# A decoder layer on one core: the first batch's work in another order, and expert 0's tokens prepared one step earlier

## What is computed

```python
h = x * rsqrt(mean(x * x) + 1e-6) * norm_w
q, k, v = heads(h @ Wq.T), heads(h @ Wk.T), heads(h @ Wv.T)   # 8 heads of 64, rope on q and k
beta, ig, og = sigmoid gates of h                             # per token and head
M = M * beta + ig * scale * outer(k, v);  y = (q @ M) * og    # scan over tokens
x = layernorm(x + y @ Wout.T + bout)
r = 0.9 * r + ctx * ctx                                       # scan over each batch's tokens
x = layernorm(x + x * r)
xn = layernorm(x) * gamma + beta                              # 8 experts, 512 tokens each
x = layernorm(x + gelu(xn @ w1[e] + b1[e]) @ w2[e] + b2[e])
```

## Time and profile before

| | us |
|---|---|
| median of 3 runs (lowest, highest) | 1338.41 (1337.49, 1339.36) |
| the profiled execution | 1336.99 |
| its span, first to last instruction | 1334.8 |
| TensorE busy | 1294.9 (97%) |
| VectorE, GpSimd, ScalarE busy | 758.3 (57%), 682.3 (51%), 506.0 (38%) |
| mean granted clock of TensorE | 0.985 |

### The profile page before, as it was taken

One profiled execution on the slowest core, in us unless ns is written; L12 is line 12 of the kernel. 1 busy time (PEld: TensorE's weight loads), 2 busy tenths in 40 slices (PEclk: granted clock), 3 DMA queues, 4 the chain that ended last, 5 costly groups with the idle time before them and its releaser, 6 DMA issues.

```text
span 1334.8 us, 17886 instructions
## 1 busy us (share of the span) xinstructions
PE 1294.9 (97%) x6330; PEld 1015.0 (76%) x6330; DVE 758.3 (57%) x1256; ACT 506.0 (38%) x723; POOL 682.3 (51%) x405
## 2 busy tenths in 40 slices
PE   4799999999999999979999999999999999999998
PEld 3677777777777777757888888888888888888886
DVE  3888888888888888883334342343333433432424
ACT  4333333333333333364343443534333434334330
POOL 1644555445455555436627438537465284375561
PEclk6899999999999999989999999999999999999999
DMA  6433322333333332413413506206125053071220
GB/s 201 137 111 112 105 91 97 104 111 111 111 111 111 111 111 81 174 47 120 165 64 130 194 0 236 88 8 252 64 95 201 26 191 131 0 260 64 68 91 31
DMA packets 108588, 150.69 MB, mean 113 GB/s; under 512 B 10112, under 2 KB 52096, under 8 KB 108544
## 3 DMA queue, kind: packets, MB, share of 16 engines
q1 hardware_dynamic: 108544, 150.10, 33.2%
HBM read 133.16 MB, written 16.92 MB: 112 GB/s over the span
## 4 chain that ended last, share of the span: by engine, by line
PE 84%; DVE 6%; issue 5%; DMA 2%; ACT 1%; POOL 0%; SPq 0%; DVEq 0%; POOLq 0%; ACTq 0%
PE qk_ps L84 8%; PE qk_ps L86 8%; PE qk_ps L85 8%; PE v_ps L84 5%; PE v_ps L86 5%; PE v_ps L85 5%; PE gate_ps L84 4%; PE gate_ps L86 4%; PE gate_ps L85 4%; PE y_ps L86 3%; PE y_ps L85 3%; PE s_ps L84 3%; PE y_ps L84 3%; PE s_ps L86 3%; PE s_ps L85 3%
## 5 line engine op out<-in xcount | busy, mean ns | idle before, releaser
L772 POOL TENSOR_TENSOR rot<-rot 128x1024 f32<-128x1024 f32 x32 | 88.3, 2758 | 188.5 <-DVE rot L951 188.5
L850 POOL TENSOR_TENSOR w_lo<-w_raw,w_hi 128x2048 fp32r<-128x2048 f32 x31 | 143.4, 4626 | 73.0 <-ACT w_hi L655 72.8
L842 POOL TENSOR_TENSOR w_lo<-w_raw,w_hi 128x2048 fp32r<-128x2048 f32 x32 | 147.8, 4619 | 20.5 <-ACT w_hi L665 20.5
L926 DVE TENSOR_TENSOR_SCAN decays<-f_all,diag 128x384 f32<-128x384 f32 x128 | 152.6, 1243 | 0.6
L1082 DVE CAST yT_hi<-v_ps 128x512 fp32r<-128x512 f32 x62 | 42.9, 692 | 182.8 <-ACT v_ps L688 182.8
L1082 DVE CAST yT_hi<-gate_ps 128x512 fp32r<-128x512 f32 x62 | 42.9, 692 | 182.0 <-ACT gate_ps L688 182.0
L84 PE MATMUL qk_ps<-wqkv_hi,xT_parts 128*128 128x512 f32 x256 | 108.2, 422 | 9.8 <-DVE wqkv_lo L888 9.8
L688 ACT ACTIVATE gate_ps<-gate_ps,b_cols 128x512 f32<-128x512 f32 x64 | 42.2, 660 | 190.4 <-PE gate_ps L86 190.4
L814 POOL TENSOR_TENSOR rstd_b<-mean_var_b,ln_eps_b 128x4 f32<-128x4 f32 x15 | 3.0, 202 | 212.6 <-DVE mean_var_b L1070 212.6
L84 PE MATMUL v_ps<-xnT_hi,w_hi 128*128 128x512 f32 x256 | 102.1, 399 | 0.0
L86 PE MATMUL qk_ps<-wqkv_hi,xT_parts 128*128 128x512 f32 x256 | 101.9, 398 | 0.0
(11 more groups left out here) (226 smaller groups left out, 3170.0 us busy)
## 6 DMA issues: line engine op xcount, KB each, us to landing
w_raw<-in_w SPq DMA_DIRECT2D x64, 1024.0 KB, 7.4
f_all<-f_dram SPq DMA_DIRECT2D x16, 1024.0 KB, 4.8
xT_raw<-in_xT SPq DMA_DIRECT2D x16, 512.0 KB, 6.0
x_both<-in_x SPq DMA_DIRECT2D x16, 512.0 KB, 4.8
f_all<-f_dram SPq DMA_DIRECT2D x16, 512.0 KB, 5.9
c_both<-in_ctx_in SPq DMA_DIRECT2D x16, 512.0 KB, 6.5
x_dram<-res SPq DMA_DIRECT2D x16, 512.0 KB, 7.3
x_both<-x_dram SPq DMA_DIRECT2D x8, 1024.0 KB, 5.3
```

What stands on the lines that cost most here:

```text
L772: pool.tensor_tensor(a, a, rot_b[j], ALU.add).then_inc(rot_done, 1)
L842: pool.tensor_tensor(w2_lo[s % 2][:], w2_raw[s % 2][:], w2_hi[s % 2][:].bitcast(F32), ALU.subtract)\
L850: pool.tensor_tensor(w1_lo[s % 2][:], w1_raw[s % 2][:], w1_hi[s % 2][:].bitcast(F32), ALU.subtract)\
L926: dve.tensor_tensor_scan(decays[:, n, :], f_all[:, n, :], diag[:], 0.0, ALU.mult, ALU.add).then_inc(decay_done, 1)
```

## The change

Start of the program. The three gate weights come as one array, as do their biases (nine DMAs for the constants, x and turned x become four ahead of the v weights, with x behind those). Batch 0's rms is not stored and read back: two matmuls against the identity (`first_rms`, behind batch 0's first v product) spread it into the free half of `gate_ps`. The q and k weights are issued right behind x, and rope's table ahead of k's. ScalarE casts v, squares x, casts q, and does the gate between the second and third k piece. In batch 0 VectorE gates v and applies rope for both halves before any scan; two scans follow, then batch 1's gate sums, then six scans and the output weights. TensorE turns batch 0's second half one share later, and its first scores another share later. GpSimd's `residual` of batch 0 stands behind both rotations, that of batch 1 at the front of step 1.

Last batches. Expert 0's tokens are loaded one step earlier, their statistics stand on VectorE between the first and second weighing of step 15, and they are normalized, turned and split in step 15, between the halves of `project_out` and behind it. Both first up products stand in the odd slots of step 16. Batch 15 uses the banks of any other batch. Tiles move with it: `xn` lies on `xT_parts0`, the first w1 slab on `f_all` (loaded behind the last scan), the second on `rot`. The order in steps 2 to 14 is as before.

```diff
-            sp.dma_start(normw[:], norm_w).then_inc(const_in, 16)
             load_xT(Step(0))
-            load_x(Step(0))
-            for g in range(3):
-                sp.dma_start(wg_raw[:, :, g * NH:(g + 1) * NH], wgT[g].rearrange("(k p) n -> p k n", p=P)).then_inc(const_in, 16)
-                sp.dma_start(gate_bias[g * NH:(g + 1) * NH, :], bg[g].rearrange("(n a) -> n a", a=1)).then_inc(const_in, 16)
+            sp.dma_start(normw[:], norm_w).then_inc(const_in, 16)
+            sp.dma_start(wg_raw[:], wgT.rearrange("(k p) n -> p k n", p=P)).then_inc(const_in, 16)
+            sp.dma_start(gate_bias[:], bg).then_inc(const_in, 16)
...
             load_w(2)
-            store_rms(Step(0))
+            load_x(Step(0))
             load_w(0)
-            spread_rms(Step(0))
+            sp.dma_start(rope_sb[:], rope.rearrange("(j p) c -> p j c", p=P)).then_inc(rope_in, 16)
             load_w(1)
+            sp.dma_start(memory_raw[:], decay).then_inc(tables_in, 16)
...
             body(Step(B - 2))
+            sp.wait_ge(xb_done, B)
+            sp.wait_ge(x2_stored, 16 * (B - 3))
+            load_tokens(Step(0))
             body(Step(B - 1))
...
-            load_w1(ahead, 0)
             sp.wait_ge(gates_turned, last.after(1, 1))
             sp.wait_ge(f_stored, last.after(16, 16))
             load_w2(ahead, 0)
+            sp.wait_ge(decay_done, last.after(NH, NH))
+            load_w1(ahead, 0)
+            sp.wait_ge(qk_turned, last.after(2 * NT, 2 * NT))
+            load_w1(ahead, 1)
+            load_w2(ahead, 1)
+            body(Step(B))
...
-                if b.n == B:
-                    expert_normalize(Step(0), 0)
-                    act.wait_ge(e_const_in, 16 * 3)
-                    token_high(Step(0), 0)
-                    token_high(Step(0), 1)
...
+                    if b.n == B - 1 and c == 2:
+                        expert_normalize(Step(0), 0)
+                    if b.n == B and c in (1, 3):
+                        gelu(Step(0), c // 2)
+                    if b.n == B and c == 0:
+                        split_w2(Step(0), 0)
                 if b.n == -1:
                     weights_high(2)
+                    square_x(b + 1)
+                    weights_high(0)
...
                 if b.n == B - 1:
+                    act.wait_ge(e_const_in, 16 * 3)
+                    token_high(Step(0), 0)
+                    token_high(Step(0), 1)
                     split_w1(Step(0), 0)
+                    token_high(Step(0), 2)
+                    token_high(Step(0), 3)
+                    keep_qkT(b, 1)
...
+                if b.n == 0:
+                    dve.tensor_tensor(gates_sum[:], gate_ps[0:NG, L:2 * L], gates_sum[:], ALU.mult).then_inc(gates_summed, 1)
...
+                    if b.n == B and n == 5:
+                        split_hidden(Step(0), 0)
+                    if b.n == B - 1 and n == 1:
+                        expert_stats(Step(0), 0)
...
                         rope_parts(b, 0)
+                        if b.n == 0:
+                            gate_v(b, 1)
+                            rope_parts(b, 1)
                         clear_f(b)
                     if b.within(B):
                         for m in SCANS.get(n, ()):
-                            if b.n != 0 or n != NH - 1:
+                            if b.n != 0 or m < 2:
                                 scan(b, m)
...
+                    for j in range(NT):
+                        add_residual(b - 1, j)
+                        if b.n == B - 1:
+                            token_low(Step(0), 2 * j)
+                            token_low(Step(0), 2 * j + 1)
+                    norm_stats(b - 1, 0)
                 if b.n == 0:
+                    for m in range(2, NH):
+                        scan(b, m)
                     weights_low(3)
...
+            def first_rms():
+                pe.wait_ge(rms_done, 1)
+                for j in range(NT):
+                    mm = pe.matmul(gate_ps[0:NG, L + j * P:L + (j + 1) * P], rms[:, 0, j:j + 1].broadcast_to([P, NG]),
+                                   ident[:], start=True, stop=True)
                 mm.then_inc(gates_ps, 1)
...
+                if b.n == 0 and g == KC:
+                    first_rms()
...
+                if b.n == B and n % 2 == 1:
+                    for k in (n // 2 * 2, n // 2 * 2 + 1):
+                        up(Step(0), k // KC, k % KC)
...
+                    if b.n == B - 2 and b.i is None and j == 1:
+                        turn_tokens(Step(0), 0)
+                        turn_tokens(Step(0), 1)
...
+                if b.n == B - 1:
+                    turn_tokens(Step(0), 2)
+                    turn_tokens(Step(0), 3)
```

186 lines of the change are left out of this document (81 added, 105 removed).

## The result

The changed kernel takes 1330.84 us, the median of 5 runs (1327.37 to 1331.16), where the kernel before took 1337.98 (5 runs, 1337.49 to 1339.36): a ratio of 0.9936, 95% interval 0.9923 to 0.9949 (the quotient of the two medians, 0.9947, lies inside it). It is faster, by 7.1 us and not by the 16 forecast, and its time lies above the range. Timed once more beside other kernels it had 1331.73 against 1338.85, ratio 0.9951 (0.9938 to 0.9964).

The account below looks back on a forecast made before the run. TensorE was taken to lose time only at the start (16.5 us idle) and the hand-over to the first expert (9.1 idle). 1336.99 − 12.2 − 4.4 = 1320.4, 1321.8 against the median, forecast 1322; range 1316 to 1329.

Parts of the forecast that it names:

- start: what goes: Batch 0's start: q-weight wait goes; v starts near 11.1, k products 20.9, projections end at 32.8 (45.55 before).
- Start: what is late next: Batch 0's second scores wait for VectorE's chain of rope, scans, gate sums and weighings: 51.5 where it was 65.10.
- rival 1: Start: VectorE blocked, all six scans at 1.85 or batch 1's rms rows late; term 1 is 7.5, 1326.5; chance 0.16.
- Term 1: Start, batch 0 and start of batch 1: 12.2 us gained, bounds 7.5 and 15.
- Term 2: Hand-over from last batches to first expert: 4.4 us gained, bounds −1 and 9.
- (a): Step 15: VectorE's statistics of expert 0's tokens delay the weighing; TensorE pays 1.5 us (0 to 3.5).
- (b): Last batches: first w1 slab, loaded later, is split on ScalarE ahead of token blocks and keys; 2.4 us (0 to 4.20).
- (c): Step 16: VectorE does batch 14's memory before weighing the second pair; costs 0.8 us.
- (d): Step 16: ScalarE's x2 scaling, w2 split and gelu table delay second value, gelu and last weighing; 3.3 us (0 to 5).
- the 12.4: Hand-over to the first expert: at most 12.4 us can come back, from 9.1 idle and about 3.3 of low clock.
- Rival 2: The end gives all back: w1 slab lands later and clock drops, term 2 is 0, 1326; chance 0.14.
- rival 4: Slower: granted clock stays at 1.2 GHz through the new order's short bursts and gaps, up to 1342; chance 0.03.

Follow-up runs that it names:

- the second profile: The changed kernel timed and profiled once more, unedited: 1331.73 against 1338.85 for the kernel before; the profiled execution took 1329.61 us.
- both edits: Changed kernel with batch 0's residual addition back between GpSimd's rotations and batch 1's sigmoid freed from waiting for the last scans: 1322.55 against 1337.59, ratio 0.9882.

## Why the prediction was wrong

**What bounds the kernel, start: what goes.** Right. v began at 12.22 for 11.1, since the v weights landed at 8.6 and not at 7.5, k at 19.97 for 20.9, the projections ended at 32.0 for 32.8. The early k is partly luck: in this execution all twelve v products ran at full clock, which only one of the nine profiles of this order without added matmuls shows; in the others k began at 21.4 to 22.6.

**Start: what is late next.** The second scores began at 51.14 for 51.5, but this agreement is luck. The sum on VectorE came out 2.8 us shorter: the low parts ended at 47.25 where it has 50.1, with six scans in 5.18 for 6.3 and gate sums in 1.2 for 2.4. What held TensorE was another path: 5.38 us of waiting before the *first* scores, because ScalarE's sigmoid of batch 1 waits for all eight scans and the keys stand behind it, and then 4.4 us of work at half clock up to the second scores, which did not wait at all. The sum has no term for the keys, and it puts 3 us of work at half clock where 4.4 ran so.

**The step that failed** is the sentence on GpSimd: "one addition follows, for which I take 3; it then has nothing until x of batch 2 arrives, whose load waits for that addition". I charged the exclusion to VectorE only, as in the rows that I had the earlier trace rows, and gave the addition its usual time; rival 1 even says that GpSimd has no work in that stretch. It took 10.04. The sentence even names who waits for it, and I didn't follow that further: no term costs x of batch 2 and the forget gates of batch 1 behind it on SyncE's queue, which is what a moved step's queue asks for. In the kernel before, that addition ended 18 us ahead of the second scores, so nothing behind it could be late; my own sum moved those scores to 51.5, and that should have sent me to look. It ends 1.7 us ahead of them now. The page of the Trainium skill that I cited, "SBUF — State Buffer" (Who interferes with whom), says that whoever issues first holds the other up for its whole instruction. The trace agrees that they exclude each other, and shows more: the addition's record starts at 39.44, ahead of the first of the six scans at 39.68 though behind the gate sum of 38.98, and the row held GpSimd up through all ten. I had turned the rule into the price of one side: "every scan that meets a GpSimd operation pays" leaves out the other order.

**Term 1** was 12.2, within the upper bound of 15, and came out as 5.9, below the lower bound of 7.5: 13.9 gained up to batch 1 and 8.0 lost behind it, 4.21 and 0.85 in waits and 2.9 by the clock. With the addition moved back, batch 2's gates come 9.7 us earlier, in an execution whose k products began at 22.64 (2.7 later than above): 12.3 without that. So term 1 would have come out near its size but for the one thing that it left out, which took more than half. The path to that size was in part another one, as said above.

**Term 2** was 4.4 and came out at 3.5. (a) 1.70 for 1.5, (b) 2.37 for 2.4, (c) nothing for 0.8, (d) 2.73 for 3.3: 6.8 for 8.0. The costs came out near the forecast or lower; what was too large is the 12.4 that "at most" comes back, which the sum takes in full, for part of the half clock stays. (The 3.3 in it is 3.1 by its own row: 7.27 us at 0.58.) From 543.86 to 615.00 the granted clock has a mean of 0.98, which over 71 us is up to 1.4.

**Sum.** Profile to profile 16.6 were forecast and 9.6 came: 6.3 short at the start, 0.9 at the end (less 0.2 outside the spans). The median lies another 2.1 off: it was 1.4 above the profiled run before and is 3.5 above it after. The clock of v's products, full in this profiled execution, can be about 2 of that, if the other executions were like the second profile; only profiled executions show that clock, so this part is argued, not shown.

**Rivals.** Rival 1 had the right place, the blocking at the start, with the wrong victim: VectorE was not the one blocked. Rival 2 did not happen. The point of rival 4, half clock behind new idle times, shows at two waits, for 4.4 and 5.8 us and not throughout, though longer than the "some 3 us" by which it was argued down. The range ended at 1329: rival 1 alone was 1326.5, and only with the 2.1 of the median and the 0.9 of the end on top of it would it have come to 1329.5.

## What to carry over

Where two engines exclude each other, cost both orders. In the kernel before they took turns and both paid; here the engine that got through paid nothing and the other the whole row of instructions. And for a step that is moved, write down who waits for its end and what stands behind that wait on the queue, two stations on; here a load of x had the next batch's gates behind it.

## What the hardware showed that I had not expected

- Ten VectorE instructions in a row, each with two inputs in SBUF, kept a GpSimd addition from running at all: 10.03 to 10.07 us in all seven profiles in which it met the row, 2.39 to 2.55 without it. With both edits, even a GpSimd addition of 128x2 elements took 3.52 us, up to the end of the row, where 0.19 is usual. An instruction without inputs between the scans changed nothing. In the kernel before, GpSimd did get in between scans: two rotations and the same addition (3.03 us) stood beside five scans, which took 1.86, 1.73, 3.07, 0.93 and 0.93 us one by one. What decides which side gets through stays open.
- The granted clock of the same twelve v products was 1.00 in one execution of the changed kernel and partly 0.50 in the next (k products from 19.97 and 21.91). Without matmuls put ahead of them they had full clock throughout in one profile of nine, with six put ahead in three of four. Ten more ahead of batch 0's first scores left the clock behind them at 1.00, where without them these take 0.80 for 0.49.
- The half clock behind a wait lasted 4.4 us behind one of 5.38, 5.8 us behind one of 4.21 and 9.6 us behind one of 2.95. Its length doesn't follow that of the wait; what sets it no run shows.
- Of the spread of 4 us between executions of the changed kernel, about 2 lie at that place. The rest goes along with the clock too: the mean granted clock was 0.993 in the execution of 1327.37, 0.988 in that of 1331.16 and 0.986 in that of 1333.35. Where in the kernel it is lost is open, as both profiles are of the fastest execution of their five.
